# A graph network's edge sums: one-hot matrices of 192 columns for a block's first and last edge tile

## The reference

```python
src = incidence[1]          # incidence = [src, dst] of the graph: here the graph's dst
dst = incidence[0]          # here the graph's src: the nodes that messages are summed at
for _ in range(3):
    msgs = relu(h[src] @ W_edge + b_edge)
    agg = segment_sum(msgs, dst, num_segments=N_NODES)
    h = relu(concatenate([agg, h], -1) @ W_agg + b_agg)
```

## Time and profile before

| | |
|---|---|
| median of 3 runs | 4232.28 us (4230.75 to 4237.94) |
| the profiled execution's own time | 4241.99 us |
| its span in the trace | 4239.9 us |
| busy: TensorE, VectorE, GpSimd, ScalarE | 87%, 76%, 68%, 53% of the span |
| mean granted clock of TensorE | 0.966 of full speed |
| tables and sort | 0 to 600 us |
| message passing, layer 1 and layer 2 | 600 to 1163 us, 1166 to 1731 us |
| last layer | 1737 to 2330 us |
| attention and feed-forward | to the end |

### The profile page before, as it was taken

The page is one execution under the profiler, slowest core; times in us unless marked ns, Lnnn a source line. Parts: engine busy times, 40 slices in busy tenths (PEclk is TensorE's granted clock), DMA queues, the critical chain, the costliest instruction groups (busy, mean ns, idle before and its releaser), DMA issues. The chain is left out here.

```text
span 4239.9 us, 101860 instructions
## 1 busy us (share of the span) xinstructions
PE 3694.8 (87%) x19862; PEld 2419.0 (57%) x19863; DVE 3215.7 (76%) x11131; ACT 2264.4 (53%) x4904; POOL 2890.5 (68%) x2867
## 2 busy tenths in 40 slices
PE   5777759999989999799999688888888769999998
PEld 3555548888778877577776344444444334444443
DVE  6888856666656766677777478888888659999998
ACT  1333325555545555465555345444454358777776
POOL 3777757776377766477663677777777377777775
PEclk8999979999999999999999899999999889999999
DMA  2555547887678877588776455555555334444443
GB/s 83 180 174 174 171 141 240 245 238 239 194 214 241 247 228 227 175 255 258 243 248 197 143 154 153 160 155 157 159 154 160 92 103 128 129 129 129 129 130 95
DMA packets 583445, 749.61 MB, mean 177 GB/s; under 512 B 146825, under 2 KB 407664, under 8 KB 583276
## 3 DMA queue, kind: packets, MB, share of 16 engines
q1 hardware_dynamic: 476652, 554.66, 40.3%
q0 software_dynamic: 106624, 193.25, 18.2%
HBM read 426.02 MB, written 321.54 MB: 176 GB/s over the span
## 5 line engine op out<-in xcount | busy, mean ns | idle before, releaser
L797 POOL DMA_INDIRECT mp_gathered<-msg_rows,other_idx x784 | 754.7, 963 | 355.2 <-issue 197.0
L1112 POOL DMA_INDIRECT ll_gathered<-msg_rows,other_idx x392 | 373.1, 952 | 221.9 <-issue 115.2
L815 PE MATMUL bank<-mp_edge_hot,mp_gathered 128*128 128x256 bf16 x3528 | 476.2, 275 | 37.2 <-POOLq L785 19.2
L559 POOL DMA_INDIRECT by_window<-so_pay,so_pos_i x392 | 387.8, 989 | 166.3 <-issue 111.8
L1698 POOL DMA_INDIRECT ff_agg<-at_rows,last_idx x392 | 382.9, 977 | 116.2 <-issue 106.9
L1403 POOL DMA_INDIRECT at_of_dst<-x_rows,node_idx x392 | 377.7, 964 | 119.4 <-issue 119.4
L1399 POOL DMA_INDIRECT at_of_src<-x_rows,kv_idx x392 | 371.9, 949 | 119.3 <-issue 97.4
L871 ACT ACTIVATE mp_h_out<-bank,mp_b_agg 128x256 f32<-128x256 f32 x392 | 185.6, 473 | 483.4 <-PE bank L833 475.7
L815 PEld LDWEIGHTS bank<-mp_edge_hot,mp_gathered 128*128 x3528 | 346.6, 98 | 107.3 <-issue 64.5
L904 DVE TENSOR_SCALAR mp_edge_hot<-digits,mp_first_col,column 128x256 bf16<-128x256 bf16 x1176 | 339.7, 357 | 69.3 <-issue 56.7
L1810 PE MATMUL bank<-ff_h_cols,ff_w 128*128 128x512 f32 x784 | 370.1, 594 | 0.9 <-ACT ff_h_cols L1843 0.9
(11 more groups left out here) (261 smaller groups left out, 8984.7 us busy)
## 6 DMA issues: line engine op xcount, KB each, us to landing
msg_rows<-mp_msg_out SPq DMA_DIRECT2D x392, 192.0 KB
mp_h_in<-h_cols SPq DMA_DIRECT2D x392, 128.0 KB
h_cols<-mp_h_out SPq DMA_DIRECT2D x392, 128.0 KB
msg_rows<-so_msg_out SPq DMA_DIRECT2D x98, 384.0 KB
h_cols<-so_h_out SPq DMA_DIRECT2D x98, 256.0 KB
ll_h_in<-h_cols SPq DMA_DIRECT2D x196, 128.0 KB
x_rows<-ll_x SPq DMA_DIRECT2D x98, 256.0 KB
skip_rows<-ll_skip SPq DMA_DIRECT2D x98, 256.0 KB
```

The source lines that it names most:

```text
L559: pool.indirect_dma_start(core.by_window, bass.IndirectOffsetOnAxis(ap=pos_i[k][:, t:t + 1], axis=0), pay[k][:, t, :], None, bounds_check= ...
L797: pool.indirect_dma_start(gathered[:, r * PARTS * D:(r + 1) * PARTS * D], None, core.msg_rows[layer % 2], bass.IndirectOffsetOnAxis(ap=cor ...
L815: product = nc.tensor.matmul(agg_bank[k], gathered[:, bass.ds(at + d * D, D)], hot, start=(first and d == 0), stop=True, skip_group_check= ...
L1112: pool.indirect_dma_start(gathered[:, r * PARTS * D:(r + 1) * PARTS * D], None, core.msg_rows[(LAYERS - 1) % 2], bass.IndirectOffsetOnAxis ...
```

## The change

The one-hot matrices and products of a block's first tile span only columns 0 to 191, those of its third tile only columns 64 to 255, and those of the middle tile all 256. The middle tile goes first, since it clears the bank. Edges of a first or third tile whose column is outside those ranges are added in the loop for further tiles.

`window_tables` finds these edges (`missed`): `place` is an edge's column within its block, and `from_1`, `from_2` and `from_3` say whether an edge's block began one, two or three tiles back or more. A second table of columns, `core.outside`, holds the column where the edge is missed or belongs to a fourth or later tile, and 65,536 more than it (so that it matches nothing) elsewhere. The loop now uses this table. A sum over all `missed` gives one flag for the whole program: if it is zero, `more_from` is 3 and the loop starts at a block's fourth tile as before; if it is above zero, `more_from` is 0, and the loop starts at a block's first tile in every block. `more_before` (how many iterations came before a block) and `passed` are made to fit, and move from `sort_by_window` into `window_tables`.

```diff
+SPANNED = ((1, 0, W), (0, 0, W - P // 2), (2, P // 2, W))
...
+            nc.vector.tensor_scalar(beyond[:, :], place[:, :], float(SPANNED[1][2]), None, ALU.is_ge).then_inc(rank, 1)
+            nc.vector.tensor_scalar(before[:, :], place[:, :], float(SPANNED[2][1]), None, ALU.is_lt).then_inc(rank, 1)
...
+            for c, table in ((1, from_1), (2, from_2), (3, from_3)):
+                nc.vector.tensor_tensor(table[:, c:NT], bank[2][:, 1:NT - c + 1], block_f[:, c:NT], ALU.is_equal).then_inc(rank, 1)
...
+            nc.vector.scalar_tensor_tensor(out=missed[:, :], in0=from_1[:, :], scalar=0.0, in1=beyond[:, :],
+                                           op0=ALU.is_equal, op1=ALU.mult).then_inc(rank, 1)
...
+            nc.vector.tensor_scalar(any_f[:, :], bank[3][0:1, 0:1], 0.0, None, ALU.is_gt).then_inc(rank, 1)
+            nc.vector.tensor_scalar(from_f[:, :], bank[3][0:1, 0:1], 0.0, float(ALWAYS), ALU.is_le, ALU.mult).then_inc(rank, 1)
+            dve.wait_ge(rank, 18)
+            nc.vector.tensor_copy(core.more_from[:, :], from_f[:, :]).then_inc(rank, 1)
+            nc.vector.tensor_scalar(more_f[:, :], core.tiles_of[:, :], from_f[0:1, 0:1], 0.0, ALU.subtract, ALU.max).then_inc(rank, 1)
...
         def further(eng, n, first, last, more):
 
-            with eng.If(first + (ALWAYS - 1) < last):
-                before = eng.value_load(core.more_before[0:1, bass.ds(n, 1)], min_val=0, max_val=NT - 1)
-                with eng.Fori(first + (ALWAYS - 1), last) as i:
-                    more(i, (before + i - (first + (ALWAYS - 1))) & 511)
+            start = first + more_from[eng.engine]
+            with eng.If(start < last + 1):
+                before = eng.value_load(core.more_before[0:1, bass.ds(n, 1)], min_val=0, max_val=NT + NW)
+                with eng.Fori(start, last + 1) as i:
+                    more(i, (before + i - start) & 1023)
...
-                        for c in range(ALWAYS):
-                            added = add_tile(r % 2, first + c, edge_hot[r % HOTS][:, c, :], first=c == 0)
+                        for c, lo, hi in SPANNED:
+                            added = add_tile(r % 2, first + c, edge_hot[r % HOTS][:, c, lo:hi], lo, hi, first=c == SPANNED[0][0])
                         added.then_inc(tile_mm[layer], 1)
                         further(pe, n, first, final, more)
...
-                            hot(more_hot[:, bass.ds((at & 1) * W, W)], n, i + 1).then_inc(more_hot_ok[layer], 1)
+                            hot(more_hot[:, bass.ds((at & 1) * W, W)], n, i, core.outside).then_inc(more_hot_ok[layer], 1)
...
-                        for c in range(ALWAYS):
-                            made = hot(edge_hot[r % HOTS][:, c, :], n, first + c)
+                        for c, lo, hi in SPANNED:
+                            made = hot(edge_hot[r % HOTS][:, c, lo:hi], n, first + c, core.column, lo, hi)
```

More of the change, by code:

```diff
@@ new lines, in _ @@
+            dve.wait_ge(chain, 12)
+            nc.vector.tensor_tensor(many[:, :], many[:, :], firsts, ALU.add).then_inc(chain, 1)
+            dve.wait_ge(chain, 13)
+            nc.vector.tensor_tensor(many[:, :], many[:, :], added, ALU.subtract).then_inc(chain, 1)
+            dve.wait_ge(chain, 14)
+            nc.vector.scalar_tensor_tensor(out=few[:, :], in0=many[:, :], scalar=any_f[0:1, 0:1], in1=few[:, :], op0=ALU.mult, op1=ALU.add).then_inc(chain, 1)
+            dve.wait_ge(chain, 15)
@@ L617, in _ @@
+            nc.vector.tensor_copy(core.passed[0:1, 0:last], few[:, :]).then_inc(chain, 1)
         @block.tensor
@@ L1121, in _ @@
             pe.wait_ge(wts, 7 * 16)
+            more_from[pe.engine] = pe.value_load(core.more_from[0:1, 0:1], min_val=0, max_val=ALWAYS)
             pe.wait_ge(parts_c, 8)
@@ L1224, in _ @@
         def _(dve):
+            more_from[dve.engine] = dve.value_load(core.more_from[0:1, 0:1], min_val=0, max_val=ALWAYS)
             nc.vector.memset(eps_col[:, :], 0.25 * EPS).then_inc(eps_ok, 1)
@@ L1239, in more @@
                     dve.wait_ge(tile_mm, at + n + 1)
-                    hot(more_hot[:, bass.ds((at & 1) * W, W)], n, i + 1).then_inc(more_hot_ok, 1)
+                    hot(more_hot[:, bass.ds((at & 1) * W, W)], n, i, core.outside).then_inc(more_hot_ok, 1)
                 first, final = edge_tiles(dve, n, r)
                 reached(dve, block_mm, n - HOTS + 1)
-                for c in range(ALWAYS):
-                    made = hot(edge_hot[r % HOTS][:, c, :], n, first + c)
+                for c, lo, hi in SPANNED:
+                    made = hot(edge_hot[r % HOTS][:, c, lo:hi], n, first + c, core.column, lo, hi)
                 made.then_inc(edge_hot_ok, 1)
```

150 lines of the change are left out of this document (96 added, 54 removed).

## The result

| | before | after |
|---|---|---|
| median of 4 runs | 4232.81 us | 7279.74 us (7277.19 to 7291.04) |
| ratio | | 1.7203, 95% interval 1.7181 to 1.7225 |
| the profiled execution's own time | 4241.99 us | 7291.04 us |
| mean granted clock of TensorE | 0.966 | 0.838 |

What follows compares the result with a forecast made beforehand. TensorE and GpSimd together were taken to set 2.51 us a block. 4242.0 + 2853 (loop, three layers) + 206 (clock) + 9 (tables) = 7310, given as 7300 us since the profiled execution ran 10 us above the median; range 6800 to 8000 us.

Steps and rivals of the forecast that it cites:

- The question that decides: Whether edges fall outside the 192 columns: 3,303 in first tiles and 2,924 in third; 587 iterations a layer, not 9.
- Rival (d): Loop stays empty because edges are ordered by column: gain of 0 to 60 us, 4180 to 4240 us; chance 0.04.
- Rival (a): Loop for further tiles bound by TensorE's sequencer: 7300 us, own range 6950 to 7700; chance 0.68.
- repeated iteration: Loop for further tiles on TensorE's sequencer: 1.12 us an iteration plus 0.28 us for the branch going back.
- The clock: TensorE idling in the three layers lowers its granted clock: 0.35 us a block, 206 us; bounds 0 and 470.
- The tables: Second table stage gets about 17 more steps, on the path: +9 us (5 to 16).
- Narrow products counted at nothing: Six of a block's nine matmuls lose 64 of 256 columns: counted as no gain, bound 94 us.
- Rival (b): Each iteration waits for a VectorE-TensorE round trip: 350 to 700 us more, 7650 to 8000 us; chance 0.15.
- The prediction's margin of 1.1 us: In the loop, VectorE's further one-hot is ready at 1.2 us, TensorE needs it at 2.3: hidden by 1.1 us.
- Rival (e): Iterations overlap more when the loop repeats, 0.8 us instead of 1.40: 700 us less, 6600 us; chance 0.08.
- Rival (c): Code loading at each of 1173 backward branches, 3 us each: 3500 us more, 10,800 us; chance 0.05.
- the 951 taken for it: Last layer's added time, taken equal to the other layers': 922 us for the loop plus 29 us for register instructions.

Runs made afterwards that it cites:

- no_loop_narrow: Changed kernel with the flag's threshold raised so the loop starts at the fourth tile, narrow spans kept, edges outside left out: 4243.68 us, ratio 1.0018.
- loop_64_columns: Changed kernel with the loop's products for further tiles spanning only columns 0 to 63: 7314.25 us.
- loop_one_part: Changed kernel with the loop multiplying one of a tile's three bfloat16 parts, one product instead of three: 6962.35 us.
- four_buffers: Changed kernel with four buffers in place of two for the further tiles' one-hots: 7252.45 us.
- loop_from_second: Changed kernel with the loop starting at a block's second tile, 391 iterations a layer instead of 587: 6420.76 us.
- loop_kept_busy: Changed kernel with four fixed-address matmuls of 256 columns added behind each further tile, into a bank nobody reads: 7161.60 us.
- half_gathers_narrow: Changed kernel with the repeated loop off, narrow spans, and every second gather left out once the ring is filled: 4236.01 us.

## Why the prediction was right

*The question that decides* was answered before any time was worked out: are there edges outside the 192 columns? 6,227 are, one flag stands for the whole program, and 1,761 iterations ran, as counted. Rival (d), the loop that stays empty, is out by the x1174 and the x587; no_loop_narrow shows what it would have brought, 4244 us, and that is not faster than before either.

*Rival (a), the sequencer-bound loop,* holds. That the array's work is off the path is shown by loop_64_columns (no iteration shorter), that the instructions are on it by loop_one_part (0.25 us for two matmuls), and that the handshake is hardly on it by four_buffers; the same products without the loop cost a seventh. The price of a block by parts, as the prediction had them and as the block at 1006.5 shows them:

| part | predicted | seen |
|---|---|---|
| entry | 1.1 us | 1.1 us |
| rest of the block | 2.3 us | 2.3 us |
| repeated iteration | 1.12 + 0.28 = 1.40 us | 1.47 us (1.461 by loop_from_second) |
| block without the clock's part | 7.3, with the register instructions 7.45 | 7.5 us |
| median block of the two layers | 7.3 + 0.15 + 0.35 = 7.8 us | 7.72 us |

The one term of the loop that was mis-sized is the repeated iteration. The step "with the gap of about 0.06 us that follows every such instruction, going back costs 0.28 us" had its branch right (221 and 228 ns), but took the loop's first instruction for part of the entry; it runs each time and costs 41 ns and the gap, about 0.1 us in starts, of which 0.07 is left. That is 1173 x 0.07 = 82 us more. The Trainium skill, "Perfetto Trace Analysis", section "Per-instruction lifecycle: what the profiler-reported window actually captures", says that only the execution of such an instruction is reported; the trace agrees once more, since this 41 ns instruction costs more than its duration in every iteration.

*The clock* was over-sized. The step "I take 0.35 for the mean, 588 x 0.35 = 206 us" rests on "TensorE idles some 4 of every 7.3 us". By the prediction's own rows its work in a block is 2.6 + 3 x 0.57 = 4.3 us, which leaves 3.0; the first layer shows (1539 - 1081) / 196 = 2.3 us idle a block. The bound of 0.8 us for a block that is slow throughout was not far off, 0.54 us by the medians of 4.72 and 4.18, but of the 352 stretches behind blocks with three iterations in the first two layers only 84 were slow throughout. Taken the other way, the layers' 3042 us less 1173 x 1.47 leave 1318 us, 2.24 a block, for all that is not a repeated iteration, where the prediction had 1417, 2.41: 0.17 us a block too much. loop_kept_busy sets the clock's price at 118 us or more, 0.20 a block, and 0.35 - 0.17 = 0.18 fits that. Granted clocks of 0.77 to 0.79 (foretold: below 0.9) say that TensorE spent a part of the time at each of its two levels.

*The errors nearly cancel,* 82 us too little and 99 us too much; that the sum came within 20 us of the measured time is luck. It is so between the layers too: with its share of the clock the prediction had 951 + 69 = 1020 us for each, and the first two came 44 and 21 us below that, the last 47 above. The tables took 5.7 us in place of 9, the sum of before's own time and the differences is 4242 + 3042 + 6 = 7290, and the profiled execution took 7291.

*Narrow products counted at nothing:* right in size, 7.4 us without the loop and 33 us with it, within the bound of 94. The reason for the first was incomplete: not only the gathers, but the sequencer too, at 2.48 us a block, stood right below the 2.51 that the narrowing attacked.

*Rival (b), the handshake,* does not set the pace: it was priced at 350 to 700 us more, and taking it away gave 27. The prediction's margin of 1.1 us for it was reckoned with 2.3 us for two iterations; by its own 1.40 it is 1.6. The rival was tempting in the rows of after, where VectorE is named ahead of 495.8 us of TensorE's idle time, more than "issue" with 381.9. The prediction's sign for right, "issue" as the largest wait ahead of the further matmuls, was only met by the weight loads (1146.4 us), and its sign for (b), "TensorE waiting for `more_hot`", did appear. Both signs were badly chosen. *Rival (e)*, iterations of 0.8 us, is out by the 1.47. *Rival (c)*, code loading on the way back, is out by the same line over both message-passing layers (median and longest branch in ns; the x1174 are all the loop's closing branches there):

```profile
L791 PEldq FUSED_REGOPS  x1174: 41/41/51, 615.4 to 3706.8; - x196
...
L791 PEldq COMPARE_BRANCH  x1174: 78/221/245, 616.5 to 3707.9; - x196
...
L791 PEldq MOVE  x392: 29/29/43, 615.3 to 3703.7; - x196
```

The longest takes 245 ns. The same rows show what was missed: `MOVE` occurs 392 times, once a block, and is the entry; `FUSED_REGOPS` occurs 1174 times, once an iteration.

The last layer cost 1067 us, 116 more than the 951 taken for it; a bound of 100 more stood beside it. The first two cost 976 and 999. Its entry and loop are no dearer (5.16 us in the mean, against 5.29 in the first two layers). The rest of the block is, with 3.22 us from the loop's last branch to the next block's branch against 2.57, since every second block, the one that also transposes a group, takes 3.9 us there.

What stays open is whether these 3.9 us are the sequencer's instructions or the array's work, and the exact worth of the clock.

## What to carry to other kernels

Before an edit is priced, count the inputs that take its exception: one flag for a whole program turns a few exceptions into all blocks, and here a saving of 0.16 us stood against an exception of some 5 us, in every block. The price of an instruction sequence on a sequencer is read from the starts of one passage, not from durations, and a passage seen once cannot say which instructions belong to the loop's head. When a wait is named in the profile, give the waiting engine more buffers and see whether the time falls by what the wait shows, before it is called the limit.

## What was not expected

- Matmuls whose operands have fixed addresses cost TensorE's sequencer almost nothing: four more to an iteration left it at 1.47 us (loop_kept_busy), whereas one with computed addresses costs 0.125 us (loop_one_part). More matmuls made the kernel faster, by 118 us.
- A named wait grew from 702 to 920 us while the time fell by 27 us (four_buffers). The one-hots that it names had been finished at least 2.6 us before they were used.
- A quarter of the columns in the loop's products made the kernel 34 us slower (loop_64_columns): no iteration became shorter, and the granted clock fell from 0.79 to 0.70.
- Products of 192 columns follow each other every 83 ns, of 256 every 109 ns; the blocks stayed at 2.48 to 2.51 us all the same (half_gathers_narrow).
- With the loop off, the changed kernel sat under three limits within 0.05 us of each other: TensorE's array at 2.51, GpSimd at 2.52 by the prediction's reckoning, and TensorE's sequencer at about 2.48 us a block. Taking one away gave 3 to 12 us; half of the gathers, the narrowed columns and the branch together are 190 us faster than the kernel before, of which some 54 are the 27 missing iterations.
